# A fused feed-forward / state-space mixer / feed-forward block on one core: four PSUM banks for the first stage's down product, products moved ahead in the first mixer's prologue, and the fifth item turned inside the last mixer

## The chip, the core and the metric

The kernel runs on one core of one Trainium2 chip. Times are microseconds (us) of device time. The engines are TensorE (PE, matmuls), VectorE (DVE), ScalarE (ACT), GpSimd (POOL) and SyncE (SP, which issues every DMA here). PE writes its results into eight PSUM banks (`banks[0]` to `banks[7]`, 128 partitions x 512 float32 each), and a bank can be written again only when ACT or DVE has read it.

## The reference, cut to what matters

Four sequences of 512 tokens, 512 wide, go through three residual steps:

```python
x = x + 0.5 * ffn(layernorm(x))
x = x + mixer(layernorm(x))
x = x + 0.5 * ffn(layernorm(x))

def ffn(x):                       # 512 -> 2048 -> 512
    x = fwht(x * SU_ug) / 64      # Walsh-Hadamard transform
    h = silu(x @ W_gate.T * s_g) * (x @ W_up.T * s_u)
    return (fwht(h * SU_dp) / 64) @ W_down.T * s_d

def mixer(x):                     # projection, 4-tap convolution, silu, then
    ...                           # a chunked state-space scan with 64 heads,
    return y @ out_proj_w.T       # gating, root-mean-square norm, projection
```

All values are float32. The kernel gets that accuracy from three passes of a matmul on a split into a high and a low part (`PASSES`: high-high, high-low, low-high).

## The kernel before, in words

The kernel has two stages that share SBUF and the eight banks. Order between engines comes only from semaphores; each engine's program is written out by hand and runs in order, so an instruction that waits holds up everything behind it on its engine.

**First stage, `begin`.** It folds the Hadamard transforms into the weights (`turn` of a "ug" or "dn" key) and runs the first feed-forward for sequences 0 and 1. A unit `n` (0 to 15) is one slice of 256 hidden features (`c = n // 2`) for one sequence (`g = n % 2`). In unit n PE runs four `up(n, j)` of 12 matmuls into banks 0 to 3, turns of weights or rows between them, through banks 6 and 7 (`T`), and then `down(n - 1)`: for each of four token tiles t, six matmuls into `D[t % 2]`, that is banks 4 and 5 (L533). DVE's `add` (L744) reads each tile's bank and adds it into `res`. `down` waits before tile t until tile t - 2 is added: `wait(pe, s_acc, TPG * n + t - 1)`. DVE's order in a unit is: low parts of the turns, `hidden`, `hidden_low`, then the four adds of unit n - 1. Unit 15 is drawn out: down(14) comes after up(15, 0), then `gate_ahead` (the gate product of slice 0 for the next stage, into bank 7), the rows of sequence 0, and down(15) in pairs.

**Second stage, `mixer`.** Six items q = 0 to 5 of eight slices b (slice number `at = 8q + b`). Items 0 to 3 each run the mixer of sequence q, and beside it a feed-forward of the sequence `beside(q) = (q + 2) % 4`; items 4 and 5 are feed-forward alone. A slice's feed-forward is `gate0`, `up0`, `gate1`, `up1` (12 matmuls each, L1160, banks F[1], F[0], F[1], F[0] = 7, 6, 7, 6) and, a slice later, `down` of four tiles (L1201). Their ACT and DVE partners are `silu`, `hidden`, `hidden_high`, `hidden_low` and `add_down` (L1746).

In the mixer of item 0 the prologue, ahead of the loop over b, is on PE: in_proj(0,1), up0(0), in_proj(0,2), gate1(0), in_proj(0,3), in_proj(0,4), products(0) (L1307), turn_b(0) (L1314), ends_out(0) (L1323), turn_d(0) (L1333). Slice 0 then goes: x_rows (L1257), four `decay` matmuls (L1247) with the halves of in_proj(0,5) between, new_states (L1285), times_start (L1292), ydiag (L1269), up1(0), from_states (L1298), in_proj(0,6), gate0(1); and slice 1: x_rows, decay, down(0, t). `decay` waits for `end_decays` on ACT (L1606), `ydiag` for the last of the decay tiles, which POOL multiplies (L2067), `from_states` for `states` on DVE (L1801 to L1807). DVE's order in slice 0: scaled, scaled_end, three times_g, hidden(0,0), hidden_low(0,0), states, conv (L1761), within (L1820), carried (L1827), hidden(0,1), hidden_low(0,1). ACT's order ahead of the loop ends with b_rows (L1601, copies turn_b's bank), gate, x_silu, end_decays. SP issues load_in(4), load_down(0), load_out(0), then waits for `aS` and moves it through HBM (`keep`), then `heads(0,0)` (L1021, L1022), and the later weights of item 0 (load_up(4) among them) inside the loop.

Rows for the next feed-forward have to be normalised, turned (transposed) on PE, split by ACT into the high part and by DVE into the low part. For the mixer of item q + 1 this is `turn_tile`, done in slice 7 of item q between the decays and the down tiles, through bank 0 into `xT`. For the feed-forward of item q + 1 it is `beside_turn` (L1148), done between items among the tiles of the last down, into `fxT`. In the boundary from item 3 to item 4, PE runs: up1(31), out_proj, then `beside_turn(4, t)` and `down(31, t)` in turn, then gate0(32), which waits for all the adds of down(31), because up1(31) must be over with `fxT` first. Item 5 goes from `xT`, turned in slice 6 of item 4.

Of the kernel before, what the change touches and what calls it, by code (L numbers as in the profile page):

```python
# [170 lines left out]
def begin(nc, s, x, wug, wsc, wdn, win, wout, cst, par, ug_s, dn_s, in_s, out_s, mid_s):  # L171
# [22 lines left out]
    with ExitStack() as ctx:  # L194
# [26 lines left out]
        U, D, T = banks[0:4], banks[4:6], banks[6:8]  # L221
# [36 lines left out]
        def halves_of(n):  # L258

            return [key for key, at in halves.items() if at[2] == n]  # L260

# [185 lines left out]
        def _(pe):  # L447
# [57 lines left out]

            def gate_ahead():

                pe.wait_ge(s_tl, turns["x", 2, TPG - 1] + 1)
                pe.wait_ge(s_wj[0], 16)
# [14 lines left out]
            def down(n, ts=range(TPG)):  # L524
# [4 lines left out]
                for t in ts:  # L529
                    wait(pe, s_acc, TPG * n + t - 1)  # L530
                    for j in range(2):
                        for i, (a, b) in enumerate(PASSES):
                            ins = pe.matmul(D[t % 2][:], hb[:, n % 2, a, j, ck(t)], wd[c % 2][:, b, j, :],  # L533
                                            start=(j == 0 and i == 0), stop=(j == 1 and i == 2))
# [14 lines left out]
            for n in range(UNITS):  # L549
                for j, keys in enumerate(unit_turns(n)):  # L550
# [4 lines left out]
                    for key in keys:  # L555
                        turn(key)
# [132 lines left out]
        def _(dve):  # L689
# [50 lines left out]
            def add(n, ts=range(TPG)):  # L740
                for t in ts:
                    dve.wait_ge(s_d, TPG * n + t + 1)
                    r = res[:, TPG * (n % 2) + t, :]
                    dve.tensor_tensor(r, D[t % 2][:], r, ALU.add).then_inc(s_acc, 1)  # L744
# [102 lines left out]
def mixer(nc, s, ug_s, dn_s, wsc, in_s, out_s, cum_m, cum_s, out):  # L847
# [17 lines left out]
    with ExitStack() as ctx:  # L865
# [56 lines left out]
        def beside_bank(i, t):  # L922

            return (S[0], S[1], A if i <= BATCH else Y, X)[t]

        def beside_to(i):

            return fxT if i < ITEMS - 1 else xT

        def opens(at):  # L930

            return at % NC == 0 and at < NC * (ITEMS - 1)

        def closes(at):

            return at % NC == NC - 1 and at != NC * (ITEMS - 1) - 1
# [17 lines left out]
        def tiles(q):  # L954
            return [res[:, TPG * q + i, :] for i in range(TPG)]
# [22 lines left out]
        def _(sp):  # L978
# [49 lines left out]
            load_in(4)  # L1028
            load_down(0)
# [7 lines left out]
            for q in range(ITEMS):  # L1037
                mix, more, other = q < BATCH, q < BATCH - 1, q < ITEMS - 1
                m0 = NIN * q + 3
                for b in range(NB):  # L1040
# [14 lines left out]
                    if not end or other:  # L1055
                        load_up(4 * at + 4)
                        load_up(4 * at + 5)
# [4 lines left out]
                    if not end or other:  # L1062
                        load_up(4 * at + 6)
# [24 lines left out]
        def _(pe):  # L1088
# [43 lines left out]
            def beside_turn(i, t):  # L1132

                mixed = min(i, BATCH)
                pe.wait_ge(s_fxn, TPG * (i - 1) + t + 1)
                if i == ITEMS - 1:
                    pe.wait_ge(s_v, BATCH)
                    pe.wait_ge(s_fxlo, TPG * (i - 1))
# [12 lines left out]
            def half_up(n, to, ks=range(KH)):  # L1151

                w, loaded, count = up_slot(n)
                frm = beside_to(n // (4 * NC))
                if ks[0] == 0:
                    pe.wait_ge(loaded, count)
                    wait(pe, s_fxlo, TPG * (n // (4 * NC)))
# [183 lines left out]
            in_proj(0, 4)  # L1341
            products(0)
# [6 lines left out]
            for q in range(BATCH):  # L1349
                more = q < BATCH - 1  # L1350
                for b in range(NB):
# [20 lines left out]
                    else:  # L1372
                        down(at - 1, 0, last_pair(q, b - 1) + 1)
                        if end and more:
# [4 lines left out]
                        if end and more:  # L1379
# [3 lines left out]
                        if end and more:  # L1383
# [8 lines left out]
                    if end and more:  # L1392
# [24 lines left out]
                if more:  # L1417
                    in_proj(q + 1, 2)
# [8 lines left out]
                if more:  # L1427
                    in_proj(q + 1, 3)
                    products(q + 1)
                    turn_b(q + 1)  # L1430
                gate0(at + 1, 0)
                if more:
                    ends_out(q + 1)
                    in_proj(q + 1, 4)
                    turn_d(q + 1)
            for at in range(NC * BATCH, NC * ITEMS):
                q, b = at // NC, at % NC
                pair = last_pair(q, b)
                if not opens(at):
                    down(at - 1, 0, last_pair(q, b - 1) + 1 if b else 0)  # L1440
                    down(at - 1, 1)
                    if q == BATCH and b == 1:
                        sums(q - 1)
                    down(at - 1, 2)
                    down(at - 1, 3)
# [13 lines left out]
        def _(act):  # L1459
# [37 lines left out]
            def beside_turn(i, t):  # L1497
                act.wait_ge(s_ftr, TPG * (i - 1) + t + 1)
# [670 lines left out]
```

## Time and profile before

| what | value |
|---|---|
| three runs | 1658.98, 1659.13, 1661.96 us, median 1659.13 |
| the profiled execution | 1660.25 us, of which its span is 1658.4 us |
| busy PE / DVE / ACT / POOL | 1628.9 / 1033.0 / 627.1 / 377.5 us |
| first stage | 0 to 341.9 us of the span |
| mixer's prologue of item 0 | 341.9 to 364.7 us |
| items 0 to 3 | 364.7 to about 1383 us |
| items 4 and 5 | about 1383 to 1658 us |

A timeline row gives the start, the length from first start to last end, the engine, the line, the operation, and the count of instructions merged in the row; in brackets stands how long the engine was idle before it and who released it. Two matmuls overlap: a single 128x512 matmul is recorded as about 0.39 us long, while its follower starts 0.227 us after it. So the length of a group of 12 is about 0.16 us more than the distance to the next group.

### The profile page before, as it was taken

The numbers are of one execution on the slowest core, as the hardware profiler recorded it, in microseconds if no ns is written. First come the engines' busy times: TensorE is split into PE (matmuls) and PEld (weight loads), VectorE is DVE, ScalarE is ACT, GpSimd is POOL, SyncE is SP. The second block draws the span as 40 slices with busy tenths as digits, with TensorE's granted clock in tenths as the row PEclk, the third lists the DMA queues.
The fourth block names the chain that finished last, engine by engine and source line by source line (L and its number), as shares of the span: only waits on it lengthen the run. The fifth ranks groups of instructions, "written<-read, shape, count | busy, mean of one in ns | idle before, by whom it ended". The sixth has DMA issues, their size and how long they took to land.

```text
span 1658.4 us, 25015 instructions
## 1 busy us (share of the span) xinstructions
PE 1628.9 (98%) x9672; PEld 1314.4 (79%) x9672; DVE 1033.0 (62%) x2022; ACT 627.1 (38%) x934; POOL 377.5 (23%) x298
## 2 busy tenths in 40 slices
PE   6999999999999999999999999999999999999999
PEld 3777777877888778888878888877888887888887
DVE  6544345766676877778777677777677664543333
ACT  4333334353433464333365333256333332122111
POOL 1656662012212212212112122121122130000000
PEclk9999999999999999999999999999999999999999
DMA  9755554645544444445535444545445546555764
GB/s 308 287 190 203 216 190 165 247 162 157 165 156 157 140 161 157 157 150 163 164 118 170 166 156 158 164 142 181 154 155 158 165 130 213 168 178 185 222 197 132
DMA packets 253427, 290.46 MB, mean 175 GB/s; under 512 B 14464, under 2 KB 211200, under 8 KB 244096
## 3 DMA queue, kind: packets, MB, share of 16 engines
q1 hardware_dynamic: 253312, 288.88, 53.0%
q8 instruction: 78, 1.28, 0.3%
q14 instruction: 37, 0.30, 0.1%
HBM read 238.51 MB, written 50.33 MB: 174 GB/s over the span
## 4 chain that ended last, share of the span: by engine, by line
PE 72%; DVE 3%; ACT 2%; issue 1%; DMA 0%; POOL 0%; SPq 0%; ACTq 0%; DVEq 0%; POOLq 0%
PE bank L1160 30%; PE bank L1201 14%; PE bank L1119 12%; PE bank L1229 5%; PE bank L1298 3%; PE bank L1269 2%; PE bank L1285 2%; PE bank L1247 2%; PE bank L1292 1%; PE bank L1257 1%; DVE res L1746 1%; DVE m_cv L1761 0%; PE bank L1148 0%; DVE xT L1720 0%; DMA cum_stay<-m_aS 0%
## 5 line engine op out<-in xcount | busy, mean ns | idle before, releaser
L1160 PE MATMUL bank<-fxT,wj 128*128 128x512 f32 x1764 | 418.8, 391 | 0.8 <-DVE res L1746 0.8
L1160 PEld LDWEIGHTS bank<-fxT,wj 128*128 128x128 f32 x1764 | 331.4, 188 | 70.3 <-DVE res L1746 1.2
L1201 PE MATMUL bank<-m_wd,m_hb 128*128 128x512 f32 x1128 | 279.2, 393 | 0.9 <-DVE m_hb L1739 0.5
L1201 PEld LDWEIGHTS bank<-m_wd,m_hb 128*128 128x128 f32 x1128 | 209.1, 188 | 45.9 <-issue 3.7
L1515 ACT CAST m_hb<-xn 128x512 fp32r<-128x512 f32 x96 | 59.5, 620 | 450.0 <-DVE xn L1733 449.9
L1119 PE MATMUL bank<-xT,wi 128*128 128x512 f32 x900 | 223.5, 396 | 1.1 <-PEq L194 0.3
L1119 PEld LDWEIGHTS bank<-xT,wi 128*128 128x128 f32 x900 | 166.9, 189 | 38.7 <-issue 3.9
L1746 DVE TENSOR_TENSOR res<-bank,res 128x512 f32<-128x512 f32 x192 | 132.6, 691 | 81.5 <-PE bank L1201 79.4
L2067 POOL TENSOR_TENSOR m_L<-m_L,m_GT 128x512 f32<-128x512 f32 x36 | 53.1, 1474 | 434.7 <-ACT m_L L1524 434.7
L1733 DVE SCALAR_TENSOR_TENSOR xn<-bank,sc,xn 128x512 f32<-128x512 f32 x96 | 71.8, 748 | 125.4 <-PE bank L1160 125.3
L1509 ACT ACTIVATE xn<-bank,sc 128x512 f32<-128x512 f32 x96 | 66.1, 688 | 145.2 <-PE bank L1160 139.7
L1524 ACT ACTIVATE m_L<-bank 128x512 f32<-128x512 f32 x128 | 76.5, 598 | 88.0 <-PE bank L1247 87.6
L1739 DVE TENSOR_TENSOR m_hb<-xn,m_hb 128x512 fp32r<-128x512 f32 x96 | 66.3, 691 | 56.9 <-ACT m_hb L1515 56.9
L533 PE MATMUL bank<-b_wd,b_hb 128*128 128x512 f32 x384 | 94.7, 396 | 2.7 <-DVE res L744 1.9
L1761 DVE SCALAR_TENSOR_TENSOR m_cv<-bank,pr,m_cv 128x511 f32<-128x511 f32 (+2 forms) x120 | 89.6, 747 | 12.1 <-ACT m_cv L1466 9.3
L502 PE MATMUL bank<-xT,b_wu 128*128 128x512 f32 x384 | 95.7, 397 | 0.0
L502 PE MATMUL bank<-b_xT,b_wu 128*128 128x512 f32 x384 | 93.0, 392 | 0.0
L1229 PE MATMUL bank<-m_wo,m_yh 128*128 128x512 f32 x384 | 90.7, 391 | 0.7 <-ACT xn L1509 0.7
L2094 POOL TENSOR_TENSOR m_ss<-m_ss,m_y 128x512 f32<-128x512 f32 x28 | 36.2, 1292 | 233.4 <-ACT m_y L1544 233.4
L533 PEld LDWEIGHTS bank<-b_wd,b_hb 128*128 128x128 f32 x384 | 70.8, 188 | 23.2 <-DVE res L744 8.1
L502 PEld LDWEIGHTS bank<-xT,b_wu 128*128 128x128 f32 x384 | 71.9, 188 | 17.8 <-issue 1.0
L1229 PEld LDWEIGHTS bank<-m_wo,m_yh 128*128 128x128 f32 x384 | 71.6, 188 | 17.7 <-issue 1.9
(224 smaller groups left out, 2312.2 us busy)
## 6 DMA issues: line engine op xcount, KB each, us to landing
wj<-ug_split SPq DMA_DIRECT2D x167, 512.0 KB, 4.3
m_wd<-dn_split SPq DMA_DIRECT2D x48, 1024.0 KB, 4.8
wi<-in_split SPq DMA_DIRECT2D x76, 512.0 KB, 3.4
ug_split<-b_wu SPq DMA_DIRECT2D x8, 2048.0 KB, 14.4
m_wo<-out_split SPq DMA_DIRECT2D x32, 512.0 KB, 4.1
wi<-ug_split SPq DMA_DIRECT2D x25, 512.0 KB, 4.2
in_split<-b_msp SPq DMA_DIRECT2D x20, 512.0 KB, 3.6
raw<-in_wug SPq DMA_DIRECT2D x8, 1024.0 KB, 6.9
```

The lines of the kernel that those rows point to most:

```text
L502: ins = pe.matmul(U[j][:], wu[c % 2][:, a, k, ck(j)], xT[g][:, b, k, :], start=(k == 0 and i == 0), stop=(k == KH - 1 and i == 2))
L533: ins = pe.matmul(D[t % 2][:], hb[:, n % 2, a, j, ck(t)], wd[c % 2][:, b, j, :], start=(j == 0 and i == 0), stop=(j == 1 and i == 2))
L1119: ins = pe.matmul(to[:], w[:, a, k, :], xT[:, b, k, :], start=(k == 0 and i == 0), stop=(k == KH - 1 and i == 2))
L1160: ins = pe.matmul(to[:], w[:, a, k, :], frm[:, b, k, :], start=(k == 0 and i == 0), stop=(k == KH - 1 and i == 2))
L1201: ins = pe.matmul(F[t % 2][:], hb[:, a, j, ck(t)], wd[:, b, j, :], start=(j == 0 and n == 0), stop=(j == 1 and n == 2))
L1229: ins = pe.matmul(F[1 - t % 2][:], yh[:, (2 * pair + i) % 4, a, ck(t)], wout[i][:, b, :], start=(i == 0 and n == 0), stop=(i == 1 and n == 2))
L1509: act.activation(hf[:, j, :], F[1][:], ACT.Silu, scale=sc[:, at % NC, j:j + 1]).then_inc(s_sil, 1)
L1524: act.activation(L[:, b % 2, j, :], A[:], ACT.Exp).then_inc(s_L, 1)
L1733: dve.scalar_tensor_tensor(hf[:, j, :], F[0][:], sc[:, at % NC, 2 + j:3 + j], hf[:, j, :], ALU.mult, ALU.mult).then_inc(s_h, 1)
L1739: dve.tensor_tensor(hb[:, 1, j, :], hf[:, j, :], hb[:, 0, j, :].bitcast(F32), ALU.subtract).then_inc(s_lo, 1)
L1746: dve.tensor_tensor(r, frm[:], r, ALU.add).then_inc(s_acc, 1)
L1761: ins = dve.scalar_tensor_tensor(cv[:, d:SEQ], frm[:, 0:SEQ - d], pr[:, w + 3 - d:w + 4 - d], cv[:, d:SEQ], ALU.mult, ALU.add)
```

## The change

Three edits, all of order and place; no arithmetic is added or taken out.

1. First stage. `D` becomes banks 4 to 7; tile t of down(n) goes into bank D[t], and in unit 15 into D[t % 3]. The wait for tile t - 2 is replaced by waits for older work: for the same tile of the unit before, and for t > 1 (banks 6 and 7) for the turns of the unit (`turned_until`). A turn now waits for the adds of down(n - 2), and `gate_ahead` for those of down(14).
2. Item 0's prologue. up1(0) moves from slice 0 (after ydiag) to right after in_proj(0,4); DVE's hidden(0,0) moves ahead to right after conv(0,1), ACT's silu(0,1) to before end_decays; gate0(1) moves from the end of slice 0 to before ydiag; load_up(4) moves on SP to right after load_in(4).
3. The fifth item (item 4) is turned by `turn_tile` in slice 7 of item 3 into `xT`, as the mixers' rows are, and gate0(32) is issued at the end of that slice, ahead of down(31). The block between items is left out after item 3, and its down(31) becomes the first of item 4's loop. Item 5 is turned into `fxT`. The statistics of item 4's rows move on DVE from slices 3 and 4 to slices 5 and 6 of item 3.

```diff
-        U, D, T = banks[0:4], banks[4:6], banks[6:8]
+        U, D, T = banks[0:4], banks[4:8], banks[6:8]
+        def down_bank(n, t):
+            return D[t] if n < UNITS - 1 else D[t % 3]
...
-            def turn(key):
+            def turn(key, after=0):
+                if 1 < after and key[:2] != ("x", 3):
+                    pe.wait_ge(s_acc, TPG * (after - 1))
...
+            def turned_until(n):
+                return turns["x", 2, TPG - 1] + 1 if n >= UNITS - 2 else max(turns[key] for keys in unit_turns(n + 1) for key in keys) + 1
...
                 for t in ts:
-                    wait(pe, s_acc, TPG * n + t - 1)
+                    if n < UNITS - 1:
+                        wait(pe, s_acc, TPG * (n - 1) + t + 1)
+                    else:
+                        pe.wait_ge(s_acc, TPG * n + max(0, t - 2))
+                    if t > 1:
+                        pe.wait_ge(s_tl, turned_until(n))
...
# SP
             load_in(4)
+            load_up(4)
             load_down(0)
             load_out(0)
...
# PE, prologue and slice 0
             in_proj(0, 3)
             in_proj(0, 4)
+            up1(0)
             products(0)
...
+                    if at == 0:
+                        gate0(at + 1, 0)
                     ydiag(q, b)
-                    if at == 0:
-                        up1(at)
                     from_states(q, b)
...
-                    if not end:
+                    if at and (not end or not more):
                         gate0(at + 1, pair + 1)
...
# PE, slice 7 of an item, and the end of item 3
-                        if end and more:
+                        if end:
                             turn_tile(q + 1, 0)
...
+                if not more:
+                    continue
                 at = NC * q + NB - 1
...
             for at in range(NC * BATCH, NC * ITEMS):
-                if not opens(at):
-                    down(at - 1, 0, last_pair(q, b - 1) + 1 if b else 0)
...
+                down(at - 1, 0, last_pair(q, b - 1) + 1 if b else NPAIR * BATCH - 1 if q == BATCH else 0)
...
# ACT
             x_silu(0, 0)
+            silu(0, 1)
             end_decays(0)
...
# DVE
             conv(0, 1, NB + 1)
+            hidden(0, 0)
             ends(0)
...
                     if at == 0:
-                        hidden(at, 0)
                         hidden_low(at, 0)
```

## Rows read from the trace of the kernel before

**Rows 1.** The page: busy time by engine, share of the span, instructions
```profile
PE 1628.9 (98%) x9672; PEld 1314.4 (79%) x9672; DVE 1033.0 (62%) x2022; ACT 627.1 (38%) x934; POOL 377.5 (23%) x298
```
**Rows 2.** PE's waits, 40 to 340 us: total, times, longest
```profile
PE bank L533 <- DVE res L744: 1.9, 8, 0.5
```
**Rows 3.** PE's timeline in the first stage
```profile
268.20 6.06 PE L533 MATMUL bank<-b_wd,b_hb 128*128 128x512 f32 x24
...
286.40 2.88 PE L533 MATMUL bank<-b_wd,b_hb 128*128 128x512 f32 x12
289.45 3.04 PE L533 MATMUL bank<-b_wd,b_hb 128*128 128x512 f32 x12 [0.16 <-DVE res L744]
...
315.13 5.60 PE L533 MATMUL bank<-b_wd,b_hb 128*128 128x512 f32 x24
320.57 8.33 PE L502 MATMUL bank<-b_xT,b_wu 128*128 128x512 f32 x36
```
**Rows 4.** DVE's timeline, the last add of the down at 286.40
```profile
292.52 0.69 DVE L744 TENSOR_TENSOR res<-bank,res 128x512 f32<-128x512 f32 x1 [0.69 <-PE bank L533]
```
**Rows 5.** PE's waits, 340 to 402 us
```profile
PE bank L1307 <- ACT m_Cf L1471: 1.8, 1, 1.8
PE bank L1269 <- POOL m_L L2067: 1.6, 1, 1.6
```
**Rows 6.** PE's timeline in the prologue and slices 0 and 1
```profile
352.95 5.60 PE L1119 MATMUL bank<-xT,wi 128*128 128x512 f32 x24
360.39 1.15 PE L1307 MATMUL bank<-m_Cf,m_GT 128*64 128x64 f32 x32 [1.84 <-ACT m_Cf L1471]
...
366.17 0.76 PE L1247 MATMUL bank<-m_mvg,m_stn 128*128 128x512 f32 x1 [0.32 <-ACT m_dc L1606]
...
372.10 1.16 PE L1285 MATMUL bank<-m_xd,m_Bt 64*128 64x128 f32 x14
...
377.09 3.79 PE L1160 MATMUL bank<-fxT,wj 128*128 128x512 f32 x12
...
388.41 2.93 PE L1201 MATMUL bank<-m_wd,m_hb 128*128 128x512 f32 x12
```
**Rows 7.** DVE's timeline in the same stretch
```profile
356.77 2.31 DVE L1761 SCALAR_TENSOR_TENSOR m_cv<-bank,pr,m_cv 128x511 f32<-128x511 f32 x3
...
374.19 1.09 DVE L1805 TENSOR_TENSOR m_sta<-m_sta,m_dc 128x128 f32<-128x128 f32 x1
...
378.77 2.31 DVE L1761 SCALAR_TENSOR_TENSOR m_cv<-bank,pr,m_cv 128x511 f32<-128x511 f32 x3
```
**Rows 8.** ACT's timeline in the same stretch
```profile
362.42 0.58 ACT L1601 COPY m_Bt<-bank 128x512 f32<-128x512 f32 x1 [1.21 <-PE bank L1314]
...
365.54 0.49 ACT L1606 ACTIVATE m_dc<-bank 128x384 f32<-128x384 f32 x1
...
376.19 0.69 ACT L1509 ACTIVATE xn<-bank,sc 128x512 f32<-128x512 f32 x1
```
**Rows 9.** Busy time, then PEclk, DMA share, GB/s, of two stretches
```profile
362.00:368.00 6.00, 5.68 (x20) 3.86 (x19) 4.72 (x9) 4.09 (x6) 0.00 (x0) 0.50 0.54 186
...
375.00:379.00 4.00, 3.72 (x69) 3.26 (x70) 3.63 (x13) 1.87 (x2) 0.13 (x1) 0.57 0.90 263
```
**Rows 10.** DMA issues on the page (count, KB, us to landing); SP's timeline
```profile
wj<-ug_split SPq DMA_DIRECT2D x167, 512.0 KB, 4.3
...
361.84 0.35 SPq L1021 DMA_DIRECT2D m_mvg<-cum_move  x1
```
**Rows 11.** PE's waits, 1350 to 1400 us
```profile
PE bank L1160 <- DVE res L1746: 0.8, 1, 0.8
PE bank L1201 <- DVE m_acc L1752: 0.4, 1, 0.4
```
**Rows 12.** PE's waits, 410 to 1250 us (three boundaries)
```profile
PE bank L1129 <- DVE xT L1720: 1.2, 6, 0.2
...
PE bank L1247 <- ACT m_L L1524: 0.6, 3, 0.2
```

More of the change, by code:

```diff
@@ L1054, in _ @@
                         load_in(m0 + 2 * (b + 2) if not end else m0 + 2 * NB + 2)
-                    if not end or other:
+                    if at:
                         load_up(4 * at + 4)
-                        load_up(4 * at + 5)
+                    load_up(4 * at + 5)
                     if mix and not end:
@@ L1061, in _ @@
                         load_in(m0 + 2 * (b + 2) + 1 if not end else m0 + 2 * NB + 3)
-                    if not end or other:
-                        load_up(4 * at + 6)
+                    load_up(4 * at + 6)
                     if 0 <= last_pair(q, b) < NPAIR * BATCH - 1:
@@ L1378, in _ @@
                         down(at - 1, 2)
-                        if end and more:
+                        if end:
                             turn_tile(q + 1, 1)
@@ L1382, in _ @@
                         down(at - 1, 3)
-                        if end and more:
+                        if end:
                             turn_tile(q + 1, 2)
@@ L1391, in _ @@
                         new_states(q, b)
-                    if end and more:
+                    if end:
                         turn_tile(q + 1, 3)
@@ L1426, in _ @@
                 down(at, 3)
[L1427 to L1430, printed above, removed]
+                in_proj(q + 1, 3)
+                products(q + 1)
+                turn_b(q + 1)
                 gate0(at + 1, 0)
[L1432 to L1435, printed above, removed]
+                ends_out(q + 1)
+                in_proj(q + 1, 4)
+                turn_d(q + 1)
             for at in range(NC * BATCH, NC * ITEMS):
@@ L1633, in _ @@
                             hidden_high(at, 0)
-                        if end and more:
+                        if end:
                             turn_tile(q + 1, j)
@@ L1651, in _ @@
                         raw(q + 1, 0, NB)
-                    silu(at, 1)
+                    if at:
+                        silu(at, 1)
                     if not end:
@@ L1920, in _ @@
                 more = q < BATCH - 1
-                other = stats(beside(q + 1), 1)
-                following = stats(q + 1, 0) if more else None
+                other = stats(beside(q + 1), 1) if more else None
+                following = stats(q + 1, 0)
                 for b in range(NB):
@@ L1929, in _ @@
                         add_down(at - 1, 0)
-                    if end and more:
+                    if end:
                         turn_tile(q + 1, 0)
@@ L1935, in _ @@
                     times_g(q, b, 0)
-                    if end and more:
+                    if end:
                         turn_tile(q + 1, 1)
@@ L1941, in _ @@
                         times_g(q, b, 1)
-                    if end and more:
+                    if end:
                         turn_tile(q + 1, 2)
```

146 lines of the change are left out of this document (72 added, 74 removed).

## The prediction

> **What bounds the kernel now.** The page first: PE is busy for 1628.9 us of a span of 1658.4 [rows 1], so only PE's own path counts; the change neither adds nor removes a matmul. All it can give is time in which PE waits, or runs at a low clock. So the next views are PE's waits by stretch, then the timelines around each wait, to see how long PE truly stood.
>
> In the first stage PE waits for the adds of the down product, 8 times, 1.9 us in all, 0.5 at most [rows 2]. The timeline tells more than that. A down of 24 matmuls that waits for nothing takes 5.44 us from its start to the next group (315.13 to 320.57) and is recorded as 5.60 long. The one at 268.20 is recorded as 6.06 long, and the row names no idle time at all. The one at 286.40 needs 3.05 us for its first 12 instead of 2.72, and its last 12 are 3.04 long instead of 2.88: about 0.45 us lost, of which the idle column holds 0.16 [rows 3]. A wait is shown as idle only once it outlasts the recorded end of the last matmul, so these waits are worth nearly three times what the wait view says. The timeline has 13 such downs, down(1) to down(13).
>
> In item 0's prologue PE waits 1.84 us for C's silu before `products` and 1.59 us for POOL before `ydiag` [rows 5], besides smaller ones, and the granted clock is 0.50 (1.2 GHz) from 362 to 368 and 0.57 on average from 375 to 379 [rows 9]; it fell after each of those two waits. up1(0) ran in the second of these stretches and took 3.79 us for what is normally 2.88 long [rows 6, 3]. At the end of item 3 PE waits twice, 0.8 and 0.4 us [rows 11].
>
> **First stage.** With four banks, tile 2 no longer waits for the add of tile 0. Eleven downs lose about 0.43 us each, 4.7 us; the two with the longest waits (0.50 and 0.44 idle, plus the same hidden 0.3) about 0.75 each, 1.5 us; sum 6.2 us. What is late next? Tile 2 now waits for the turns of its unit. DVE does the low parts of these before any add, so the new wait is over no later than the one it replaces. The turn of the next unit waits for the four adds, and behind it on PE stand all the `up`s: the last add of the down at 286.40 starts at 292.52 and ends at 293.21 [rows 4], the turn comes only after the 12 matmuls of `up`, 2.7 us behind down's end at 292.3, so it has 1.8 us in hand. Each unit gets 0.43 us shorter for DVE, ACT, POOL and the DMA queue as well; over the whole span DVE is busy for 62% and the others for less [rows 1], so I charge nothing. Bounds: 1.9 us, if the idle column were the whole of it, and 6.5 us. I take 6.2, because the start-to-start distances are measured and not modelled ends.
>
> **Prologue of item 0.** Worked from rows, in order. in_proj(0,4) ends at 358.55. up1(0) needs hidden(0,0), which DVE runs after the convolution that ends at 359.08: 0.74 us, so PE starts at 359.8 after a wait of 1.2, and up1 takes 2.73: 362.5 [rows 6, 7]. products (1.1) and turn_b (0.6) end at 364.2. ACT then goes in order: from b_rows' start to end_decays' end it took 3.6 us (362.42 to 366.03), and silu(0,1) now stands in front of end_decays, 0.7 more [rows 8]: about 368.6, where before it was 366.1. So PE's first decay is 2.5 us later than before, and waits about 2 us for it. Moving up1 (2.73 us) ahead has gained almost nothing up to there: the waits are as long, elsewhere, and one of them is new.
>
> From the first decay to new_states took 5.9 us (366.17 to 372.10), 1.1 of it from the low clock; at full clock 4.8, so new_states starts at about 373.4 and ends at 374.6. gate0(1), 2.7 us, then stands where PE waited 1.59 for POOL; POOL's tile is ready by about 375.6, under cover of it. If gate0(1) were not there the wait would come back. ydiag comes to 378.8. Its neighbour from_states waits for DVE's `states`, which ran from 373.87 to 378.77 before, with one operation at 1.09 us beside a POOL multiplication [rows 7]; 4.2 to 5.0 us, so it ends at 378.8 to 379.6, about where it ended before. From there DVE and ACT, and no longer PE, set the pace: convolution, within and carried 3.6 us, hidden(0,1) 0.75, its high part on ACT 0.65, its low part 0.7: down(0,0) at 385.3 in place of 388.41 [rows 6]. PE's own work (from_states, in_proj(0,6), x_rows, a decay) would be over at 384.6, so a new wait of some 0.7 us stands before down(0,0). hidden(0,0) no longer lies on DVE ahead of `states`, which is half of why this comes out ahead. Gain: 3.1 us at full clock.
>
> *The clock.* The new order still holds a stretch, about 364 to 369, of small products and of 2 us of waiting; it fell in such a stretch before [rows 9]. If it falls there once, the halves of in_proj(0,5) cost 0.8 to 1.4 us more, and states moves with them: gain 2.0. If states takes 4.2 us and the clock stays, 3.9. In no case more than the waits named in [rows 5] plus what the low clock took (6.0 x 0.50 + 4.0 x 0.43 = 4.7 us, [rows 9]), 8.1 us. I take 2.9, between the two clock cases and nearer to full clock, since the first fall followed the 1.84 us wait, which is shorter now and followed by dense work.
>
> The Trainium skill (TensorE: Matmul & The Clock Gate, HAM oscillation) speaks of the clock as lost only through waits longer than any in this prologue. The trace disagrees: waits of 1.84 and 1.59 us, with small products around them, were enough. By the page's rule the new order would stay at full clock; that is the first rival below.
>
> *SP.* load_up(4) goes ahead of load_down(0), load_out(0), keep(0) and heads(0,0). It is issued when up0(0) is over, adds about 0.5 us of issue and 512 KB that land in about 4.3 us; the heads were issued at 361.84 [rows 10] after a wait for `aS`, not for the queue, and are now needed 2.5 us later. At zero; at most 1 us, if the extra transfer pushes `keep`'s small packets back by more than that slack. load_up(5) stays where it was.
>
> **Item 4.** down(31)'s first tile no longer follows right behind out_proj (0.44 idle), and gate0(32) no longer waits for the last add of down(31) (0.78 idle) [rows 11]; with the hidden 0.3 of each, 1.7 us. Against it, the transposes in slice 7 cost what they cost at the three other boundaries: an idle 0.2 for a decay and 0.2 twice for the low part of `xT` [rows 12], with the hidden parts 1.0 us. The 16 transposes are the same number in both orders. The other new load of slice 7, four low parts on DVE (2.5 us) ahead of `states`: PE has up0, gate1 and ydiag to cover it, 6.5 us against about 6.2, so 0 to 0.5. Sum: gain 0.7, between -0.5 and 1.7.
>
> **Sum.** 6.2 + 2.9 + 0.7 = 9.8 us. Against the profiled execution (1660.25, its span 1658.4 and 1.85 around it) that is 1650.4. That execution stands 1.1 us over the median of the runs, 1659.13, so the number for the median is 1649.3; some of the 1.1 may be clock that the median run did not lose and cannot get back, so I say 1649.5.
>
> **Rivals.**
> - *The clock stays at full speed* through the new prologue, and states is quick: prologue 3.9 to 5, time 1648. For it: up1 and gate0 fill the two waits after which it fell. Against: the new wait for end_decays.
> - *The prologue only moves its waits*: the ACT order (b_rows, gate, x_silu, silu, table load, end_decays) costs the 2.5 us and the clock falls during the dense halves and again before down(0,0); gain 0 to 1, time 1652. For it: up to the first decay my sum already finds no gain.
> - *The idle column is right*: the longer steps of the down tiles are a property of going from one bank to another and stay; first stage 1.9, time 1653.8. Against: down(14), the same two banks, shows none of them [rows 3].
> - *The first stage becomes bound by the crossed waits*: a turn waits for the adds of down(n - 2), a down tile for the turns. From the point where DVE's last add comes over 1.8 us later than now, all `up`s behind the turn wait. At 1 us a unit, 14 units: the 9.8 turn into -4, time 1663.5, slower than before. Against: DVE has slack in every unit, and the add pace is set by PE [rows 4].
> - *The change does not do what it says in item 4*, since the boundary's waits come back at slice 7: gain -0.5, time 1650.7; that is inside the range of the forecast.
>
> **How the numbers follow.** Forecast (about 1647.5 to 1651.5) 0.55; full clock 0.15; moved waits 0.15; idle column 0.10; slower rival 0.03; other 0.02. Predicted time 1649.5. The range takes in the first rival and the second with run-to-run scatter, 1645.5 to 1654.0. A measurement of this kernel can tell about 0.2%, 3.3 us, from no change: faster is anything below 1655.8. Of the cases only a part of the idle-column one together with a failed prologue comes out between 1655.8 and 1662.4. Faster 0.90, same 0.06, slower 0.04.
>
> **What would show it.** The wait of L533 for L744 gone and every down 5.44 us long start to start; the turns without a wait; up1(0) at 359.8 (counted from the old start of this stage) and about 2.9 long; a wait for end_decays of about 2 us; none before ydiag; down(0,0) with a short wait for `hidden_low`; the decay and `xT` waits four times, not three, and no wait at gate0(32). The prediction is wrong if the downs keep their longer steps, if the stretch of item 0 to down(0,0) is not 2 us shorter, or if a wait on a turn appears.

## The result, and the profile after

Before 1659.92 us, after 1656.9 us (medians of 17 runs each, taken side by side). The ratio is 0.9978, 95% interval 0.9971 to 0.9985: faster by some 3.7 us (2.5 to 4.8), where 9.8 were forecast. The direction was right; the time stands 2.9 us above the top of the forecast's range. The profiled execution of after took 1658.09 us, its span 1656.2.

PE again, first on the page of after (busy us, share of the span, instructions), against [rows 1]:

```profile
PE 1621.9 (98%) x9672; PEld 1311.9 (79%) x9672; DVE 1033.3 (62%) x2022; ACT 626.5 (38%) x934; POOL 377.0 (23%) x298
```

PE's recorded busy time fell by 7.0 us with the same 9672 matmuls, but the span by 2.2. So waits hidden in modelled lengths went, and others came that show as idle. PE's waits in the first stage of after, 40 to 340 us (total, times, longest), against [rows 2]:

```profile
PE bank L489 <- POOL parts L428: 1.7, 2, 0.9
PE bank L495 <- DMA draw<-down_half: 1.2, 1, 1.2
```

The wait for `add` is gone, and one on POOL's low parts of the weights has come. (The 1.2 on `draw`, a transfer ahead of down(1), is 0.3 in stage1_alone and counts with the start, below.) In the prologue, 340 to 402 us, against [rows 5]:

```profile
PE bank L1271 <- ACT m_dc L1626: 1.6, 1, 1.6
PE bank L1225 <- DVE m_hb L1759: 1.4, 1, 1.4
PE bank L1184 <- DVE xn L1753: 1.2, 1, 1.2
PE bank L1271 <- ACT m_L L1544: 0.7, 1, 0.7
PE bank L1281 <- ACT m_xc L1494: 0.6, 1, 0.6
PE bank L1322 <- DVE m_sta L1827: 0.6, 1, 0.6
PE bank L1140 <- DVE m_cv L1781: 0.5, 1, 0.5
```

The 1.8 and 1.6 of [rows 5] are gone; 1.6 for `end_decays`, 1.4 ahead of down(0,0) and 0.5 for the convolution are new, as is the 1.2 that up1(0) now waits for hidden(0,0); the three others are small. At the end of item 3, 1350 to 1402 us, against [rows 11]:

```profile
PE bank L1184 <- issue: 1.4, 1, 1.4
PE bank L1150 <- DVE xT L1740: 0.4, 2, 0.2
PE bank L1271 <- ACT m_L L1544: 0.2, 1, 0.2
```

Both old waits went, three small ones came as forecast, and one of 1.4 that was not: its releaser is not shown ("issue"), and it has to be looked up on SP (below).

For each edit a segment of the timeline can be measured from the start of one matmul group to that of another (the last column: to the start of the last matmul), so that modelled lengths play no part. This table is used for every experiment (us):

| kernel | down(1) to second stage | second stage to down(0,0) | item 3, ydiag of slice 6, to the end |
|---|---|---|---|
| before | 257.81 | 46.43 | 315.88 |
| after | 253.80 | 44.86 | 317.53 |
| stage1_alone | 254.08 | 47.08 | 315.91 |
| prologue_alone | 257.71 | 46.38 | 315.98 |
| item4_alone | 257.93 | 46.16 | 317.51 |
| after_again | 254.07 | 46.31 | 317.44 |
| sp_order | 254.00 | 44.83 | 315.88 |
| halves_first | 251.23 | 47.60 | 317.31 |
| prologue_reordered | 253.79 | 46.45 | 317.88 |
| high_before_gate | 253.66 | 45.74 | 317.69 |
| stage1_and_halves | 251.24 | 46.48 | 316.01 |
| all_three | 251.23 | 44.34 | 315.79 |
| load_ahead | 251.24 | 44.33 | 315.93 |

Before against after: first stage -4.0, prologue -1.6, item 4 +1.65, together -3.9. Between the second and the third segment a further 1.1 went, 1.0 of it because a wait for `m_stn` at the start of item 3, which comes and goes between executions, was in before and not in after. And 2.9 came: down(1) starts at 87.05 in place of 84.18, 1.9 of it already there at PE's first matmul (11.37 against 9.44, waiting for the first load). Added up that is -2.2 (unrounded), as the spans have it. The 2.9 belong to this execution: over the traces of all thirteen executions told of here, PE's first matmul starts between 9.2 and 11.4, down(1) between 83.4 and 87.1, and stage1_alone, with the same first stage as after, had 9.23 and 84.47. The median of the runs agrees with the three segments.

### The profile page after: what moved, and what is told of

The parts are those of the page before. It is cut to its first block, busy times and chain, and to the rows that moved or that the text cites. A ratio compares the mean times of both kernels' runs of the same rounds, so it can differ in the third digit from the quotient of the medians.

```text
span 1656.2 us, 25046 instructions
## 1 busy us (share of the span) xinstructions
PE 1621.9 (98%) x9672; PEld 1311.9 (79%) x9672; DVE 1033.3 (62%) x2022; ACT 626.5 (38%) x934; POOL 377.0 (23%) x298
## 3 DMA queue, kind: packets, MB, share of 16 engines
q8 instruction: 78, 1.28, 0.3%
## 4 chain that ended last, share of the span: by engine, by line
PE 72%; DVE 4%; ACT 2%; issue 1%; DMA 0%; SPq 0%; ACTq 0%; DVEq 0%
PE bank L1184 30%; PE bank L1225 14%; PE bank L1140 12%; PE bank L1253 5%; PE bank L1322 3%; PE bank L1293 2%; PE bank L1309 2%; PE bank L1271 2%; PE bank L1316 1%; PE bank L1281 1%; DVE xT L1740 0%; DVE m_cv L1781 0%; DVE res L1766 0%; PE bank L1168 0%; PE bank L1150 0%
## 5 line engine op out<-in xcount | busy, mean ns | idle before, releaser
L1766 DVE TENSOR_TENSOR res<-bank,res 128x512 f32<-128x512 f32 x192 | 132.5, 690 | 83.4 <-PE bank L1225 81.2
L1781 DVE SCALAR_TENSOR_TENSOR m_cv<-bank,pr,m_cv 128x511 f32<-128x511 f32 (+2 forms) x120 | 89.6, 747 | 11.4 <-ACT m_cv L1489 8.6
L549 PE MATMUL bank<-b_wd,b_hb 128*128 128x512 f32 x384 | 90.9, 392 | 0.0
L508 PEld LDWEIGHTS bank<-b_xT,b_wu 128*128 128x128 f32 x384 | 72.1, 188 | 16.3 <-issue 0.7
```

Of the source, the lines that this page charges most:

```text
L508: ins = pe.matmul(U[j][:], wu[c % 2][:, a, k, ck(j)], xT[g][:, b, k, :], start=(k == 0 and i == 0), stop=(k == KH - 1 and i == 2))
L549: ins = pe.matmul(down_bank(n, t)[:], hb[:, n % 2, a, j, ck(t)], wd[c % 2][:, b, j, :], start=(j == 0 and i == 0), stop=(j == 1 and i == 2))
L1766: dve.tensor_tensor(r, frm[:], r, ALU.add).then_inc(s_acc, 1)
L1781: ins = dve.scalar_tensor_tensor(cv[:, d:SEQ], frm[:, 0:SEQ - d], pr[:, w + 3 - d:w + 4 - d], cv[:, d:SEQ], ALU.mult, ALU.add)
```

## The experiments

All ratios are against before, on the same chip, with 95% intervals.

**Each edit alone.** First stage alone (cut; the crossed waits of the turns are in it too):

```diff
-        U, D, T = banks[0:4], banks[4:6], banks[6:8]
+        U, D, T = banks[0:4], banks[4:8], banks[6:8]
...
-                    wait(pe, s_acc, TPG * n + t - 1)
+                    if n < UNITS - 1:
+                        wait(pe, s_acc, TPG * (n - 1) + t + 1)
...
```

> Kernel before with the first stage's edit alone (four banks, crossed waits). Theory: the down tiles' waits on the adds go (6.2 us, start to start, from down(1) to down(13)), but the turn of the down weights after the first up of every second unit now waits for POOL's low part, which stands on POOL behind the blocks of mixer weights; four such waits of 0.07 to 1.1 us, so 3.5 to 4.5 us less than before, and 1.5 to 3 us of waits of that turn on POOL in the first stage. Rival (the forecast as it stood): that wait belongs to one disturbed execution only; then no wait of a turn on POOL, and 6.2 us less than before.

Measured: 1656.15 us, 0.9976 [0.9966, 0.9986]. The segment gained 3.7. The waits of its first stage, 40 to 340 us, name the cause of what is missing from 6.2:

```profile
PE bank L489 <- POOL parts L428: 2.2, 2, 1.2
```

The prologue alone (PE's part; ACT, DVE and SP are changed as in edit 2):

```diff
# PE
             in_proj(0, 4)
+            up1(0)
             products(0)
...
+                    if at == 0:
+                        gate0(at + 1, 0)
                     ydiag(q, b)
-                    if at == 0:
-                        up1(at)
```

> Kernel before with the edit of item 0's prologue alone (up1(0), hidden(0,0), silu(0,1), gate0(1), load_up(4)). Theory: from the start of the second stage to the first matmul of down(0,0) it takes 44.8 us at full clock where before took 46.4 with two low-clock stretches, so 1.5 us less; in runs in which the clock falls also here, 0 to 1 less. Rival (the forecast): 43.3 us, 3 us less, since after the states only DVE's chain counts and not ACT's queue, in which the gate waits for in_proj(0,6).

Measured: 1661.6 us, 1.0009 [1.0001, 1.0018]. The segment is 46.38 against 46.43 of before: nothing. PE's waits, 341 to 402 us, are those of after to the tenth:

```profile
PE bank L1248 <- ACT m_dc L1608: 1.6, 1, 1.6
PE bank L1202 <- DVE m_hb L1743: 1.4, 1, 1.4
PE bank L1161 <- DVE xn L1737: 1.2, 1, 1.2
```

So the 1.5 us between this execution and after is not in the waits; it is the clock (below). The whole runs are even 0.2 to 3.0 us slower than before; the profiled one was the third fastest of eleven, and what made the others longer was not traced.

Item 4 alone:

```diff
-                        if end and more:
+                        if end:
                             turn_tile(q + 1, 0)
...
+                if not more:
+                    continue
                 at = NC * q + NB - 1
```

> Kernel before with the edit of the fifth item alone. Theory: the two waits at the end of item 3 go (1.7 us with their hidden parts), the decay and xT waits come a fourth time (1.0), and up1(32) waits about 1.4 idle us (1.7 start to start) for its weights, whose load stands on SP behind load_down(32) and so behind the end of down(31): 0.5 to 1.5 us slower than before. Rival (the forecast): no wait ahead of up1(32), 0.7 us faster.

Measured: 1661.59 us, 1.0007 [0.9998, 1.0016]; the segment 1.6 us longer, with the same wait as in after, in a trace that has nothing else of the change (the whole runs alone, -0.3 to 2.7 us, would not settle it):

```profile
PE bank L1167 <- issue: 1.4, 1, 1.4
```

**The same kernel again**, to learn what an execution of it scatters by. No edit.

> The changed kernel once more, unedited, for a second trace of it. Theory: the same waits in the same places (turn on POOL in the first stage 1.5 to 3 us, down(0,0) on hidden_low about 1.4, up1(32) about 1.4), time 3 to 4.5 us less than before; only the first 70 us, whose transfers start late by up to 3 us, and the clock in the prologue differ from the first trace. Rival: the waits were of that one execution, and this trace shows others.

Measured: 1657.34 us, 0.9987 [0.9978, 0.9996], just outside the first interval, though the two intervals overlap; together they put the gain between 2 and 4 us. Its prologue took 46.31, that of after 44.86, with the same order of the same instructions. The windows from 366 to 370 us (busy PE, PEld, DVE, ACT, POOL; PEclk, DMA share, GB/s; PEclk 1.00 is 2.4 GHz, 0.50 is 1.2 GHz), first of after, then of after_again:

```profile
366.00:370.00 4.00, 2.08 (x8) 1.44 (x8) 3.07 (x6) 2.32 (x4) 0.00 (x0) 1.00 0.37 150
```

```profile
366.00:370.00 4.00, 3.08 (x7) 2.48 (x8) 2.50 (x5) 1.36 (x3) 0.00 (x0) 0.57 0.31 125
```

One more kernel, halves_first (below), had 0.57 over the eight microseconds from 362, and the longest segment of all, 47.60:

```profile
362.00:370.00 8.00, 7.31 (x24) 4.92 (x26) 3.53 (x6) 2.70 (x5) 0.00 (x0) 0.57 0.03 11
```

At full clock the new prologue takes 44.8 to 44.9 (after, sp_order); when the clock falls for some 3.4 us, as in prologue_alone and after_again, 46.3 to 46.4, no better than before; when for 7 us, 47.6. But before had the low clock for longer. Its whole segment, then that of after:

```profile
341.99:388.41 46.42, 41.98 (x272) 33.44 (x273) 33.04 (x64) 27.49 (x36) 9.64 (x11) 0.89 0.54 176
```

```profile
340.85:385.70 44.85, 38.17 (x272) 30.00 (x273) 33.04 (x64) 27.87 (x37) 9.65 (x11) 1.00 0.53 173
```

What is not busy is PE's waiting: 4.4 us in before, 6.7 in after. The busy time goes with the clock in all thirteen traces, whatever the order: 38.2 us at a mean PEclk of 1.00 (two traces), 39.4 to 39.7 at 0.96 (four), 40.4 to 40.9 at 0.92 to 0.93 (three), 41.8 to 42.1 at 0.89 (four). So the new order waits 2.2 us longer than before, and its gain is clock alone. The four traces with the old order have 0.89 to 0.93, the six with the prologue's edit (high_before_gate, with one exchange on ACT, among them) 0.93 to 1.00; none shows the old order at full clock, so whether the new order brings the better clock about is not shown.

The whole runs scatter with the clock too: of the 17 of after, the three with a mean granted clock of 1.000 have spans of 1652.4 to 1653.0, the four with 0.996 of 1656.6 to 1657.4.

**SP's order at the end of item 3.** The `issue` wait stands before up1(32), the first product that reads `wi`. PE's timeline of after, and SP's, around it (start, length; SPq rows are DMA issues):

```profile
1382.35 5.64 PE L1184 MATMUL bank<-xT,wj 128*128 128x512 f32 x24
1389.39 5.73 PE L1184 MATMUL bank<-xT,wi 128*128 128x512 f32 x24 [1.41 <-issue]
```

```profile
1374.33 0.82 SPq L1028 DMA_DIRECT2D m_wo<-out_split  x2
1382.54 0.32 SPq L1022 DMA_DIRECT2D m_wd<-dn_split  x1
1382.90 1.48 SPq L1017 DMA_DIRECT2D wi<-ug_split  x2
```

The load into `wi` is issued at 1382.90, right behind load_down(32) at 1382.54, and that waits for the end of down(31), since it overwrites its weights. up1(32) starts 6.5 us after its load was issued; in before it was 8.7 us (issued at 1383.20, started at 1391.87), with no wait. In before the whole of down(31) ran ahead of gate0(32); now gate0(32) is ahead of it, and up1(32) comes only two products behind the down that its load has to wait for. The edit puts the load ahead of the one that waits:

```diff
+                if q == BATCH - 1:
+                    load_up(4 * NC * (q + 1) + 3)
                 if other:
                     load_down(NC * (q + 1))
...
-                if mix:
+                if more:
                     load_up(4 * NC * (q + 1) + 3)
```

> The changed kernel with one line of SP moved: after item 3 the load for up1(32) is issued ahead of load_down(32), which waits for the end of down(31). Theory: the 1.4 us wait of PE before up1(32) goes and the stretch from the last ydiag but one to the end shortens from 317.5 to 315.8 us, 1.7 us faster than the changed kernel. Rival: that wait is for HBM or for the transfer itself and stays; no change.

Measured: 1656.27 us, 0.9978 [0.9969, 0.9987]. In its SP timeline the load leaves 7.3 us ahead of load_down:

```profile
1374.89 0.52 SPq L1017 DMA_DIRECT2D wi<-ug_split  x1
1382.24 0.32 SPq L1022 DMA_DIRECT2D m_wd<-dn_split  x1
```

and all that PE waits for from 1350 to 1402 us is

```profile
PE bank L1152 <- DVE xT L1742: 0.4, 2, 0.2
PE bank L1273 <- ACT m_L L1546: 0.2, 1, 0.2
```

The segment is 315.88, exactly that of before. The queue was the whole of the +1.65; without it the edit is worth nothing, not the 0.7 of the forecast. The ratios of whole runs can't tell this kernel from after (both 0.9978); that rests on the segments, 317.3 to 317.9 in six traces with the old order on SP and 315.8 to 315.9 in three with the new one.

**The order of the weights' halves.** In after's first stage, PE's and POOL's timelines at one of the two waits:

```profile
195.67 5.62 PE L549 MATMUL bank<-b_wd,b_hb 128*128 128x512 f32 x24
201.13 2.88 PE L508 MATMUL bank<-b_xT,b_wu 128*128 128x512 f32 x12
204.93 0.70 PE L489 MATMUL bank<-parts,b_Hr 128*128 128x512 f32 x2 [0.93 <-POOL parts L428]
```

```profile
201.00 2.56 POOL L421 TENSOR_TENSOR b_msp<-b_mraw,b_msp 128x512 fp32r<-128x512 f32 x2 [7.56 <-ACT b_msp L631]
203.52 1.27 POOL L428 TENSOR_TENSOR parts<-draw,parts 128x512 fp32r<-128x512 f32 x1
```

The down takes its 5.46 us; but the turn after `up` needs the low part that POOL finished at 204.79, and in front of that stood two blocks of the next stage's weights (L421), for which POOL had idled 7.56 us, until ACT had done their high part. The edit, on both engines, puts the halves that PE needs next ahead of these blocks:

```diff
# POOL
+                    for key in halves_of(2 * c + g + 1):
+                        low_half(key)
                     if c:
                         low_block(4 * (c - 1) + 2 * g)
                         low_block(4 * (c - 1) + 2 * g + 1)
-                    for key in halves_of(2 * c + g + 1):
-                        low_half(key)
# ACT
-                high_blocks(n)
                 for key in halves_of(n + 1):
                     high_half(key)
+                high_blocks(n)
```

> The changed kernel with, in the first stage, the high and low parts for the turned weights ahead of the blocks of mixer weights in ACT's and POOL's order. Theory: the waits of the turn on POOL (2.2 us idle, 2.6 start to start) go; from down(1) to the second stage 251.3 us in place of 254.0, 2.5 us faster than the changed kernel. Rival: POOL is bound by something else in its chain (the butterflies, the load of the raw weights) and the wait stays or moves to another turn; 253 to 254 us.

Measured: 1654.29 us, 0.9966 [0.9954, 0.9979], with a low clock for 7 us of the profiled prologue. POOL's timeline of it shows the order turned round:

```profile
159.20 2.54 POOL L428 TENSOR_TENSOR parts<-raw,parts 128x512 fp32r<-128x512 f32 x2
164.62 2.54 POOL L421 TENSOR_TENSOR b_msp<-b_mraw,b_msp 128x512 fp32r<-128x512 f32 x2 [2.89 <-ACT b_msp L631]
```

PE's only wait from 40 to 334 us is `PE bank L484 <- DVE last L711` with 0.3, and the segment is 251.23: 6.6 us shorter than before. The same order with the first stage's edit and neither of the other two, stage1_and_halves:

> Kernel before with the first stage's edit and the halves ahead of the blocks, and neither the prologue's edit nor item 4's. Theory: 6.5 us less than before (down(1) to the second stage 251.3 us), so that the other two edits, even mended, are worth 1 to 2 us. Rival: the mended prologue and item 4 carry half of the 7.8 us; then this one is only 4 us under before.

Measured: 1653.23 us, 0.9957 [0.9945, 0.997], segment 251.24. That the spans (1651.8 and 1658.4) also differ by 6.6 is partly luck: a start 1.0 later and the wait for `m_stn`, absent here, nearly cancel. The new order without the four banks wasn't run; before has no wait on POOL there [rows 2] that it could take away.

**Another order in the prologue.** silu(0,1) earlier on ACT, so that `end_decays` is not behind it; hidden(0,0) back from the head of conv(0,1); the second half of the slice's features earlier on DVE and ACT:

```diff
# ACT
             raw(0, 1, NB + 1)
+            silu(0, 1)
             sums_high(0)
...
             x_silu(0, 0)
-            silu(0, 1)
             end_decays(0)
# DVE
             step_rest(0)
+            hidden(0, 0)
             step_out(0)
...
             conv(0, 1, NB + 1)
-            hidden(0, 0)
...
                     scaled_end(q, b)
+                    if at == 0:
+                        hidden(at, 1)
...
                         hidden_low(at, 0)
+                        hidden_low(at, 1)
                     states(q, b)
```

> The changed kernel with the partners of up1(0) earlier: silu(0,1) on ACT right after raw(0,1), hidden(0,0) on DVE in its idle time after step_rest, hidden(0,1), its high and its low part before the states of slice 0. Theory: the wait before up1(0) (1.25 us), part of the one for end_decays (0.65) and the one before down(0,0) (1.4) go; from the start of the second stage to down(0,0) 42 to 43 us at full clock, in place of 44.9. Rival: the chain over b_rows, x_silu and end_decays or the states sets down(0,0) anyway, and the wait comes back in front of x_rows or from_states: 44 us or more.

Measured: 1656.51 us, 0.9977 [0.9968, 0.9986]. Of the waits from 334 to 400 us those ahead of up1(0), from_states and down(0,0) are gone, that for `end_decays` is shorter, and one on a transfer is new:

```profile
PE bank L1140 <- DMA wi<-in_split: 1.7, 1, 1.7
PE bank L1271 <- ACT m_dc L1626: 1.1, 1, 1.1
```

The segment is 46.45, with the clock low for some 10 us of it (mean PEclk 0.89). PE waits 4.5 us in it, against 6.7 in after, and is busy for 41.9 against 38.2: the shorter waits are there, and the clock took more than they gave. An estimate for full clock, 38.2 + 4.5 = 42.7 us, lies in what was expected; no trace shows it.

**One instruction in the prologue.** In after, three rows tell why down(0,0) waits: PE and ACT,

```profile
380.57 3.01 PE L1140 MATMUL bank<-xT,wi 128*128 128x512 f32 x12 [0.54 <-DVE m_cv L1781]
...
385.70 2.97 PE L1225 MATMUL bank<-m_wd,m_hb 128*128 128x512 f32 x12 [1.45 <-DVE m_hb L1759]
```

```profile
383.62 0.60 ACT L1513 ACTIVATE m_zs<-bank 128x512 f32<-128x512 f32 x1 [2.53 <-PE bank L1140]
384.11 0.61 ACT L1535 CAST m_hb<-xn 128x512 fp32r<-128x512 f32 x1
```

and DVE:

```profile
381.53 0.74 DVE L1753 SCALAR_TENSOR_TENSOR xn<-bank,sc,xn 128x512 f32<-128x512 f32 x1
384.75 0.69 DVE L1759 TENSOR_TENSOR m_hb<-xn,m_hb 128x512 fp32r<-128x512 f32 x1 [2.49 <-ACT m_hb L1535]
```

hidden(0,1) was ready at 382.27, but its high part stood on ACT behind `gate`, which waited 2.53 for in_proj(0,6), which had waited for the convolution. The edit: the high part ahead of the gate.

```diff
                         x_silu(q, b + 1)
+                        if at == 0:
+                            hidden_high(at, 1)
                         gate(q, b + 1)
                     elif more:
                         b_silu(q + 1)
-                    hidden_high(at, 1)
+                    if at:
+                        hidden_high(at, 1)
```

> The changed kernel with two instructions of ACT exchanged in slice 0: hidden_high(0,1) ahead of gate(0,1), which waits for in_proj(0,6). Theory: the 1.4 us wait of PE before down(0,0) is ACT's queue and goes; at full clock down(0,0) starts 43.4 to 43.6 us after the second stage's start in place of 44.85, which is what the forecast had (43.3). Rival: the wait belongs to DVE's chain after the states, which the forecast named; then at least 0.7 us of it stays.

Measured: 1656.41 us, 0.9976 [0.9966, 0.9985]; the wait before down(0,0) fell from 1.45 to 0.79, and the segment, 45.74, is 0.6 shorter than in the two traces of the old ACT order with the same clock (0.96; 46.31 and 46.38). Why not to nothing, DVE's and POOL's timelines of this kernel tell:

```profile
381.15 1.80 DVE L1762 TENSOR_TENSOR m_hb<-xn,m_hb 128x512 fp32r<-128x512 f32 x1 [0.69 <-ACT m_hb L1535]
```

```profile
379.88 1.16 POOL L2102 TENSOR_TENSOR m_y<-m_y,m_ex 128x448 f32<-128x448 f32 x1 [7.22 <-DVE m_ex L1850]
381.12 1.28 POOL L2104 TENSOR_TENSOR m_y<-m_y,m_zs 128x512 f32<-128x512 f32 x1
```

The low part took 1.80 us where it takes 0.69, beginning 0.03 after a POOL operation of 1.28: it ends 0.55 after that one. The Trainium skill (SBUF — State Buffer, "SBUF: two separate sides") says that VectorE, with two inputs in SBUF, and GpSimd take a shared pair of ports as an exclusive lock, the later one waiting for the whole instruction of the other. The trace agrees in the main: 1.25 until the POOL operation is over and 0.55 behind it make 1.80. A full 0.69 behind it would make 1.94; the rows don't say where the 0.14 went.

**All together.** sp_order, halves_first and the reordered prologue in one:

> The changed kernel with all three of the other edits. Theory: the gains add, 1.7 + 2.5 + 2 us, about 1651 us, 8.5 us or 0.5% under before. Rival: the gains overlap or fall to the clock in the prologue: 1653 to 1655 us.

Measured: 1652.06 us, 0.9953 [0.9941, 0.9966]; 251.23, 44.34 and 315.79. Of the prologue's waits the one for `wi` remained (1.5), so the last kernel has that load ahead of `keep`:

```diff
+            load_in(5)
             keep(0)
             heads(0, 0)
-            load_in(5)
             load_in(6)
```

> The kernel with all three other edits, and load_in(5) on SP ahead of the wait for aS. Theory: the 1.5 us wait of in_proj(0,5) on its weights goes and is replaced by nothing larger: down(0,0) 1 to 1.5 us earlier than without it at the same clock, 1651 us, 0.55% under before. Rival: the transfer of 512 KB delays the small packets of keep, so that the first decay waits for them: no gain.

Measured: 1650.17 us, 0.9931 [0.9918, 0.9945]: the best, some 11 us under before and 7 to 8 under after. The wait for `wi` went, and in the waits from 334 to 400 us another stands at the top:

```profile
PE bank L1273 <- DMA m_stn<-cum_stay: 1.6, 1, 1.6
```

That is the small transfer of `heads(0,0)`, behind `keep`, which the load now stands ahead of: it leaves SP 23.2 us after the second stage's start, against 22.3 in all_three. So the rival is true in part. The segment (44.33) is that of all_three (44.34), but not at the same clock: 0.92 against 0.96. PE waits 3.9 us in place of 4.9 and is busy for 40.4 in place of 39.4, so at one clock the move would be worth about 1 us (an estimate). The intervals of the two kernels overlap slightly; that load_ahead owes all of its last 0.2% to this move is not shown.

## Why the prediction was wrong

**First stage: the size was right, the step "so I charge nothing" failed.** That the downs lose three times what the idle column holds is shown: with four banks down(1) to down(12) take 5.44 to 5.46 us from start to start in after (down(13) 5.76, for a reason that its rows don't name), and with the halves in order the stage is 6.6 us shorter, where 6.2 were worked out and 1.9 was the idle column's. That rival is out. The failing step took DVE 62% busy and the others less [rows 1] for a reason that none of them falls behind. POOL is busy for 23% and still came late, since its order put two blocks, for which it waits on a transfer and on ACT, ahead of the half that PE needs next. [rows 2] names no wait on POOL, but the trace of before shows how thin the cover was:

```profile
164.81 1.28 POOL L424 TENSOR_TENSOR parts<-draw,parts 128x512 fp32r<-128x512 f32 x1
```

```profile
166.24 0.70 PE L483 MATMUL bank<-parts,b_Hr 128*128 128x512 f32 x2
```

POOL's part ends at 166.09, 0.15 ahead of the turn, and where PE does wait, in after, the turn also starts 0.14 behind it: nothing was in hand here. At the same turn of three other units it ended 0.4, 0.6 and 1.1 ahead. Twice in the stage PE now stands for it, 1.7 us in the idle column and 2.6 from start to start: 4.0 in place of 6.6. The wait on a turn was named as a sign of a wrong prediction, but was looked for at DVE's adds, where there is none: the crossed waits of the fourth rival cost nothing.

**Prologue: right up to from_states, wrong behind it, and the clock.** The rows of after, against the steps, counted from the second stage's start (340.85):

```profile
358.66 3.02 PE L1184 MATMUL bank<-fxT,wj 128*128 128x512 f32 x12 [1.25 <-DVE xn L1753]
...
367.52 0.47 PE L1271 MATMUL bank<-m_mvg,m_stn 128*128 128x512 f32 x1 [1.64 <-ACT m_dc L1626]
...
376.59 1.10 PE L1293 MATMUL bank<-m_L,m_xp 128*32 128x64 f32 x64
378.25 1.77 PE L1322 MATMUL bank<-m_Cf,m_sta 128*128 128x64 f32 x14 [0.56 <-DVE m_sta L1827]
```

up1(0) came at 17.8 (forecast 17.8, from 359.8), the first decay at 26.7 (26.6), from_states at 37.4 (between 36.8 and 37.6), no wait before ydiag. down(0,0) was forecast at 43.3 and came at 44.86. The step that failed is the last one, "a new wait of some 0.7 us": it had in_proj(0,6) run behind from_states without a wait, and hidden's high part on ACT behind nothing. In the trace in_proj(0,6) waits 0.54 for the convolution's read of its bank, ACT's gate waits for in_proj(0,6), and the high part waits for the gate; that makes the wait 1.45. high_before_gate shows about half of that term (0.66 of the wait); the rest of its gain went to DVE's 1.80. What is left of the 3.1 at full clock is 1.6. And that is not from waits: PE waits 6.7 us in this stretch, where before waited 4.4, so the step "moving up1 ahead has gained almost nothing up to there" holds for the whole prologue, and the 1.6 is the clock that before had lost.

The clock was taken as falling in some executions, at 1.1 us. It is 1.5 (44.86 and 46.31, same kernel), which takes all of the gain: prologue_alone, with it fallen, is as long as before. Five executions of the prologue as changed (after, after_again, prologue_alone, sp_order, halves_first) average 46.0, between 44.8 and 47.6; four of before's order (before, stage1_alone, item4_alone, stage1_and_halves) 46.5, between 46.2 and 47.1. So the second rival, that the prologue only moves its waits, is nearest. It forecast 0 to 1 us; the 0.5 between these means is less than their scatter, and the runs of prologue_alone show no gain. The stretch after the wait for `end_decays` fell to half clock in some executions and not in others (0.57 and 1.00 above). In the old order it fell 1.3 us behind the wait of 1.84 in before, and only some 7 us behind the same wait in item4_alone. By the rule that the prediction cites from the Trainium skill (TensorE: Matmul & The Clock Gate, HAM oscillation) it would stay at full clock; after bears it out, and after_again doesn't.

**Item 4: the step for PE was right, the one for SP was missing.** The waits that the forecast named went, the three small ones came (0.2 each, as in [rows 12]). The sum was a little off as it stood: with the hidden 0.3 of each wait the two old ones make 1.8 and not 1.7, the three new ones 1.5 and not 1.0, which leaves 0.3. But what the edit took from behind down(31), gate0(32) with its 2.7 us and the wait of 0.8 ahead of it, was cover for a transfer. The prediction weighed SP for load_up(4), which the diff moves, and not for the load of up1(32), whose text the diff leaves alone, but whose user moved. It cost 1.65, and sp_order took away 1.65. What remains is nought: from x_rows of slice 7 to the first down of item 4 it took 47.49 us in before and 47.01 in sp_order, so 0.5 is there, but in_proj(3,18) in slice 6 comes 0.3 later, and the last 0.2 is scatter of this segment (315.8 to 316.0 in seven traces). The rival that the item 4 edit doesn't do what it says gave -0.5, 1.1 short.

**The sum.** 4.0 for 6.2, 0 to 1.6 for 2.9, -1.65 for 0.7: 2.3 to 4.0 in all, measured 3.7 (after) and 2.2 (after_again). Of the missing 6 us or more, 2.4 lie with item 4, 2.2 with the first stage, and 1.3 to 2.9 with the prologue. The first two are queues whose order the diff does not touch there. The range was too narrow because no case in it had a wait on POOL or on SP's queue, and each rival was taken by itself, where three terms came short at once.

Open: why the clock falls in some executions of the same instructions and not in others; how much of load_ahead's lead over all_three is the moved load (its profiled execution, span 1650.6, was the slowest of five, and all_three's, 1649.9, the second fastest); and what moves the start by up to 2 us.

## What to carry to other kernels

When an edit brings a consumer forward, go through every producer in program order, even one that is a fifth busy, and ask what stands ahead of the item it needs and what that waits for; a transfer whose code is not in the diff can still be the one that is late. A wait or a product that goes from one place may have been the cover of another wait: price what comes second. Measure waits on PE from start to start: the idle column held a third of what one bank pair cost. And where the clock moves, compare waits and busy time apart: a segment that got shorter may wait longer.

## What the runs showed of the hardware

- A 128x512 VectorE operation of 0.69 us took 1.80 beside a GpSimd one of 1.28 that began 0.03 earlier.
- The granted clock from 366 to 370 us was 1.00 in one execution and 0.57 in another of the same kernel: 1.5 us of the span.
- The same matmuls kept PE busy for 38.2 us at full clock and for 41.8 to 42.1 at a mean granted clock of 0.89, over thirteen traces with several orders.
- PE waits of up to about 0.3 us leave no idle time in the rows: 6.6 us of the first stage against 1.9 recorded.
- The first matmul started between 9.2 and 11.4 us, whatever the kernel.
